# One group of attention value products is placed later in its cycle of steps

## The chip, the cores and the metric

The program runs on one core of one Trainium2 chip. The metric is the device time of one execution in microseconds (us), as the median of several runs. Lower is better.

## The reference, cut to what matters

Four blocks follow each other, each on a layer-normed input and with a residual: causal attention with ALiBi, a mixture-of-experts feed-forward on part of the rows, causal attention with rotary embedding, and the feed-forward again. Both attentions have 4 batches of 2048 rows of 256 features, 16 heads of 16. All is f32.

```
q, k, v = (x @ W.T + b), split into 16 heads of 16
scores  = q @ k.T * scale (+ alibi), masked to be causal
out     = softmax(scores) @ v           # the value products
x       = x + out @ Wo.T
```

Only the order in which one piece of `softmax(scores) @ v` is issued changes here. What is computed stays the same.

## The kernel before, in words

Each attention layer and batch (8 in all, "beta") has 16 heads, worked on as 8 pairs. So there are 64 head pairs, g = 0 to 63. One head pair is one pass over 36 steps, n = 0 to 35, in nine cycles of four steps. A pass takes about 54 us.

In one step and for one pair g, the following happens.

- **unit(g + 1, n)** on TensorE (PE, lines 1226, 1232 and 1239) multiplies queries by keys for the *next* head pair, both heads at once in the two halves of the array's rows. VectorE (DVE, line 1594) takes the row maxima out of PSUM. The products go to two pairs of banks in turn, so unit n waits (semaphore `p1_used`) until DVE has reduced unit n - 2. After unit 35 DVE also makes the negated maxima (lines 1601 to 1613).
- **score(g, n, u)** for u = 0 and 1 (lines 1196, 1200 and 1205) multiplies keys by queries for this head pair, with the maxima folded in. Each uses one bank of a ring of three, so it waits (`ring_used`) until the result three places before it has been taken out. ScalarE (ACT, line 1081) writes the exponential of it to `probs`.
- **times_v(g, group)** (line 1263), the value products, multiplies `probs` by the values of the steps of a group and adds them up in one PSUM bank, `ps_acc`. It waits for the last exponential of its group.
- After the last group of a block of 512 queries (qt) ACT copies `ps_acc` to `acc_sb` (line 1092, `acc_evac`), and SyncE's queue (SP) stores that copy with four DMAs (line 826, `store_o`). The first group of the next block waits for the copy (`acc_out`).

Steps run from qt = 3 down to qt = 0. The value groups are pairs of steps, and triples at the end of a block: group 14 is steps 30, 31 and 32 and ends block qt = 1; group 15 is steps 33, 34 and 35 and is the whole of block qt = 0. `value_slots` gives each group one of two value places per cycle, numbered k: the first place of a cycle is even, the second odd. Group 14 has place 16 and place 17 is empty; group 15 has place 18, which is place 0 of the next head pair.

Cycles are written out by hand in two orders. Where the cycle has a job for the ring (a projection, a transpose, an output product), which is so for the last cycle in 57 of the 64 head pairs, the last cycle on PE is, with n = 32:

```
unit 32; score(32,0); job; unit 33, masks first; score(32,1); score(33,0)
unit 34; score(33,1); PLACE 16; unit 35, masks first
score(34,0); score(34,1); score(35,0); PLACE 17; score(35,1), masks first
```

Without a job (g = 0, 57 and 59 to 63) it is:

```
unit 32; score(32,0); score(32,1); score(33,0); unit 33; PLACE 16
score(33,1), masks first; score(34,0); unit 34; score(34,1); score(35,0)
unit 35; score(35,1); PLACE 17
```

"Masks first" means that the small bf16 matmuls with the causal mask stand ahead of the large ones of that item. ACT goes through its exponentials in the same order, with the copy (`value_evac`) at the matching place: place 16 lies after exp(33,1), place 17 between exp(35,0) and exp(35,1) with a job and after exp(35,1) without. All engines run their own instruction list in order and wait on semaphores. After head pairs 31 and 60 (`EX_AFTER`) the experts' feed-forward follows, with group 15 ahead of it; after 63 comes the tail of the kernel.

Of the kernel before, what the change touches and what calls it, by code (L numbers as in the profile page):

```python
# [134 lines left out]
def value_slots():  # L135

    ready = [CYCLE * c + half for c in range(CYCLES + 1) for half in range(2)]
    found, k = {}, 0
    for i, steps in enumerate(GROUP):
        while ready[k] < steps[-1]:  # L140
            k += 1
        found[k], k = i, k + 1
    return found


GROUP_AT = value_slots()
assert len(GROUP_AT) == GROUPS and GROUP_AT[2 * CYCLES] == GROUPS - 1 and 0 not in GROUP_AT
LAST_GROUP = {qt: max(i for i, steps in enumerate(GROUP) if STEP[steps[0]][0][0] == qt) for qt in range(NQ)}
# [6 lines left out]
EX_AFTER = (NG // 2 - 1, NG - 4)  # L155
# [191 lines left out]
def build(nc, x_in, w_a, wo_a, bqk_a, bv_a, bo_a, w_b, wo_b, tri_in, ramp_in, cos_t, sin_t, rows_in_t,  # L347
# [12 lines left out]
    with ExitStack() as ctx:  # L360
# [219 lines left out]
        def evac_index(g, qt):  # L580
            return NQ * g + NQ - 1 - qt
# [5 lines left out]
        def step_width(n):  # L587
            return sum(QW - q0 for _, _, q0, _ in STEP[n])
# [37 lines left out]
        def _(sp):  # L626
# [189 lines left out]
            def store_o(g, qt):  # L816
                e = evac_index(g, qt)
                beta, p = divmod(g, PAIRS)
                sp.wait_ge(acc_out, e + 1)
                for u in range(2):  # L820
                    row = o_d[beta % 2, 2 * p + u, :, qt * QW:(qt + 1) * QW].rearrange("r (c n) -> r c n", n=P)
                    for inner in range(2):
                        to = row[:, 1:3, :] if inner else row[:, 0::3, :]
                        tile = 32 * (2 * u + inner)
                        src = acc_sb[tile:tile + DH + 1, e % ACCS, :].rearrange("p (c n) -> p c n", n=P)
                        sp.dma_start(to, src).then_inc(o_st[e % ACCS], 16)
# [27 lines left out]
            def experts(ly):  # L854
                sp.wait_ge(pv_mm, GROUPS * (EX_AFTER[ly] + 1))
                load_w2(w2_sb[0], expert_at(0), ew2_in[0])
                sp.wait_ge(qk_split, 2 * (unit_index(EX_UNITS[ly], NQ - 1, CH - 1) + 1))
                e = expert_at(1)
                load_w1(w1_sb[1], e, ew1_in[1])
                load_w2(w2_sb[1], e, ew2_in[1])  # L860
                sp.wait_ge(h_mm, (ly * ETILES + 1) * NF)
                sp.dma_start(xb[:, :, :], x_raw.rearrange("(t p) d -> p t d", p=P)).then_inc(xb_in, 16)
                for i in range(2, ETILES):
                    sp.wait_ge(h_mm, (ly * ETILES + i - 1) * NF)
                    e = expert_at(i)
                    load_w1(w1_sb[i % 2], e, ew1_in[i % 2])
                    sp.dma_start(xs_sb[:, i % 2, 0:HALVES[i], :], slots(xs, i)).then_inc(xs_in[i % 2], 16)
                    sp.wait_ge(fy_mm, halves_to(ly, i - 1))
                    load_w2(w2_sb[i % 2], e, ew2_in[i % 2])
                    store_ys(ly, i - 2)  # L870
                store_ys(ly, ETILES - 2)
                store_ys(ly, ETILES - 1)
# [32 lines left out]
            for g in range(NG):  # L905
                if g % PAIRS == 0 and g // PAIRS == B - 1:
                    sp.wait_ge(job_mm, JOB_PLACE[("v", B - 1, NQ - 1, CH - 1)] + 1)
                    sp.wait_ge(next_stored, 32)
                    for i, w in enumerate((wqkv, wqkv_low)):
                        sp.dma_start(w[:, :, :].bitcast(F32), w_d[i].rearrange("p (k n) -> p k n", k=KD))\  # L910
                            .then_inc(weights_in, 16)
                if g % PAIRS == 0 and g // PAIRS == B + 1:
                    sp.wait_ge(job_mm, JOB_PLACE[("y", B - 1, NQ - 1, CH - 1)] + 1)
                    sp.dma_start(wo[:, :, :], wo_b.rearrange("(k p) n -> p k n", p=P)).then_inc(wo_in, 16)
                for n in range(STEPS):
                    for j in JOBS[g][n]:
                        job(*j)
                    if g < NG - 1 and n % 2 == 0 and n >= 2 and GROUP_AT.get(n // 2 - 1) in LAST_QT:
                        store_o(g, LAST_QT[GROUP_AT[n // 2 - 1]])
                    if n == 2 and g and g - 1 not in EX_AFTER:  # L920
                        store_o(g - 1, 0)
                if g in EX_AFTER:
                    store_o(g, 0)
                    experts(EX_AFTER.index(g))
            job("zo", LAST, 3, 0)
# [878 lines left out]
```

## Time and profile before

| | us |
|---|---|
| runs, median of 3 | 3925.78 (3919.76 to 3927.37) |
| the profiled execution, time | 3912.85 |
| its span, first to last instruction | 3911.0 |
| PE busy / weight loads (PEld) busy | 3804.0 / 2394.0 |
| DVE busy / ACT busy | 2954.7 / 2759.7 |
| mean granted TensorE clock | 0.995 |

Durations below come from the profiled execution. Busy times overlap between engines. A busy PE is not PE at its peak, since the ends of matmuls are modelled.

### The profile page before, as it was taken

Reading aid. Unit: us, or ns where it says so; the run is one execution under the profiler, and the core shown is the slowest. Engines: PE = TensorE matmul, PEld = TensorE weight load, DVE = VectorE, ACT = ScalarE, POOL = GpSimd, SP = SyncE. Lnnn points to the kernel's source line nnn. Section 1 sums busy time; section 2 is a strip of 40 time slices with the busy share of each in tenths; the row PEclk is TensorE's granted clock in tenths of the full one; section 3 lists DMA queues with packets and bytes.
Section 4 is the critical chain, followed back from the end, with each engine's and each line's share of the span. In section 5 each row is a group of like instructions: output and inputs, shape, how many; then the busy total and the mean of one; then the engine's idle time right before and its main releaser. Section 6 shows DMA issues by size and latency. Waiting matters only on the chain.

```text
span 3911.0 us, 109334 instructions
## 1 busy us (share of the span) xinstructions
PE 3804.0 (97%) x42693; PEld 2394.0 (61%) x42693; DVE 2954.7 (76%) x3839; ACT 2759.7 (71%) x5702; POOL 1062.0 (27%) x1794
## 2 busy tenths in 40 slices
PE   7999999999999999999999999999999999999998
PEld 5555555655665655556875565655656555557955
DVE  8888888888888888885048888888888888883075
ACT  2777777777777777776257777777777777774265
POOL 4121112222222234442024433333343332120021
PEclk9999999999999999999999999999999999999999
DMA  5333233224333343335644334344333333336622
GB/s 165 77 76 92 56 79 91 73 77 97 78 87 92 93 114 94 92 104 170 229 138 117 95 89 102 92 105 105 90 99 99 83 90 89 73 83 196 232 68 83
DMA packets 275748, 407.05 MB, mean 104 GB/s; under 512 B 65226, under 2 KB 190098, under 8 KB 262418
## 3 DMA queue, kind: packets, MB, share of 16 engines
q1 hardware_dynamic: 272158, 391.66, 37.7%
q0 software_dynamic: 3072, 8.39, 0.8%
q8 instruction: 337, 5.52, 0.6%
q14 instruction: 181, 1.48, 0.1%
HBM read 264.70 MB, written 122.13 MB: 99 GB/s over the span
## 4 chain that ended last, share of the span: by engine, by line
PE 50%; DVE 2%; ACT 2%; issue 1%; SPq 1%; DMA 1%; POOL 0%; ACTq 0%; DVEq 0%
PE ps_acc L1263 14%; PE ps_r L1200 10%; PE ps_p L1232 9%; PE ps_p L1388 4%; PE ps_r L1400 4%; ACT probs L1081 2%; PE ps_r L1324 2%; DVE part_max L1594 1%; PE ps_r L1205 1%; PE ps_r L1309 1%; PE ps_p L1226 1%; PE ps_r L1319 1%; PE ps_r L1310 1%; PE ps_r L1311 1%; PE ps_p L1239 1%
## 5 line engine op out<-in xcount | busy, mean ns | idle before, releaser
L1594 DVE TENSOR_REDUCE part_max<-ps_p 128x2 f32<-128x1024 f32 (+3 forms) x2560 | 2623.1, 1060 | 567.6 <-PE ps_p L1232 375.8
L1081 ACT ACTIVATE probs<-ps_r 128x512 f32<-128x512 f32 (+1 forms) x4608 | 2333.9, 575 | 684.9 <-PE ps_r L1200 430.5
L1200 PE MATMUL ps_r<-q_stack,k_stack 54*128 54x512 f32 (+3 forms) x5120 | 1378.4, 392 | 37.9 <-ACT probs L1081 29.1
L1232 PE MATMUL ps_p<-k_stack,q_stack 52*128 52x512 f32 (+3 forms) x5120 | 1246.7, 427 | 20.2 <-DVE part_max L1594 17.7
L1263 PE MATMUL ps_acc<-probs,v_head 128*17 128x256 f32 x19456 | 1145.1, 360 | 1.8 <-ACT probs L1081 1.6
L1200 PEld LDWEIGHTS ps_r<-q_stack,k_stack 54*128 54x128 f32 x5120 | 733.4, 187 | 268.1 <-ACT probs L1081 219.5
L1263 PEld LDWEIGHTS ps_acc<-probs,v_head 128*17 128x17 f32 x19456 | 488.8, 97 | 467.5 <-issue 219.3
L1232 PEld LDWEIGHTS ps_p<-k_stack,q_stack 52*128 52x128 f32 x5120 | 557.8, 186 | 288.2 <-DVE part_max L1594 143.9
L1205 PE MATMUL ps_r<-id,mk 64*128 64x64 bf16 x3598 | 284.3, 194 | 0.0
L1715 DVE COPY xf<-ps_r 128x256 f32<-128x256 f32 x46 | 19.5, 424 | 316.1 <-PE ps_r L1400 316.1
L1032 POOL TENSOR_TENSOR bk<-bk,y_sb 128x256 f32<-128x256 f32 x104 | 76.4, 735 | 647.8 <-ACT y_sb L1132 647.7
L986 POOL TENSOR_TENSOR swp<-swp,cs 128x256 f32<-128x256 f32 x128 | 91.2, 735 | 546.2 <-ACT probs L1081 330.2
L1145 ACT ACTIVATE hid_f<-ps_p 128x256 f32<-128x256 f32 (+1 forms) x240 | 80.3, 334 | 220.6 <-PE ps_p L1388 220.6
L1205 PEld LDWEIGHTS ps_r<-id,mk 64*128 64x128 bf16 x3598 | 158.9, 95 | 87.6 <-issue 46.9
L995 POOL CAST pa<-tmp 128x512 fp32r<-128x512 f32 x128 | 78.6, 614 | 483.8 <-ACT tmp L1123 451.3
L1003 POOL CAST x_high<-xT 128x512 fp32r<-128x512 f32 x56 | 34.3, 612 | 599.3 <-ACT xT L1111 599.3
L998 POOL TENSOR_TENSOR pb<-tmp,pa 128x256 fp32r<-128x256 f32 x256 | 182.4, 734 | 10.3
L1400 PE MATMUL ps_r<-probs,hid_f 128*128 128x256 f32 x736 | 164.0, 379 | 1.1 <-issue 1.1
L1239 PE MATMUL ps_p<-id,mk 64*128 64x64 bf16 x2196 | 164.6, 195 | 0.0
L1092 ACT ACTIVATE acc_sb<-ps_acc 128x256 f32<-128x256 f32 x256 | 99.5, 389 | 76.9 <-PE ps_acc L1263 69.4
L1309 PE MATMUL ps_r<-x_high,wqkv 128*128 128x256 f32 x448 | 149.5, 334 | 0.0
L1400 PEld LDWEIGHTS ps_r<-probs,hid_f 128*128 128x128 f32 x736 | 137.6, 190 | 19.1 <-issue 1.3
(199 smaller groups left out, 3157.2 us busy)
## 6 DMA issues: line engine op xcount, KB each, us to landing
q_stack<-parts SPq DMA_DIRECT2D x378, 128.0 KB
k_stack<-parts SPq DMA_DIRECT2D x378, 128.0 KB
parts<-pa SPq DMA_DIRECT2D x128, 256.0 KB, 2.8
parts<-pb SPq DMA_DIRECT2D x128, 256.0 KB, 3.5
probs<-w_dram SPq DMA_DIRECT2D x30, 1024.0 KB, 6.1
o_sums<-acc_sb SPq DMA_DIRECT2D x1008, 17.0 KB
swp<-tmp SPq DMA_DIRECT2D x128, 128.0 KB, 3.3
bk<-recips SPq DMA_DIRECT2D x58, 256.0 KB
```

Of the source, the lines that this page charges most:

```text
L998: pool.tensor_tensor(pb[:, at % 2, h], x[:, h], pa[:, at % 2, h].bitcast(F32), ALU.subtract)\
L1081: act.activation(probs[:, at % PBUF, u, 0:w], block_bank(g, n, u)[:, 0:w], ACT.Exp)\
L1092: act.activation(acc_sb[:, e % ACCS, :], ps_acc[:, 0:D], ACT.Copy).then_inc(acc_out, 1)
L1200: mm = pe.matmul(bank[:, col:col + QW - q0], ks[s][r, kb * P:(kb + 1) * P], qs[s][r, qt * QW + q0:(qt + 1) * QW], start=fresh, stop=True, ...
L1205: mm = pe.matmul(bank[:, lo:lo + HALF], mk[half, 2 + part % 2, :], id64[half, :], start=False, stop=True, skip_group_check=True)
L1232: mm[u] = pe.matmul(banks[:, u, col:col + w], qs[s][r, qb * P:(qb + 1) * P], ks[s][r, kc * QW:kc * QW + w], start=fresh, stop=True, skip_g ...
L1239: mm[u] = pe.matmul(banks[:, u, lo:lo + HALF], mk[r, part % 2, :], id64[r, :], start=False, stop=True, skip_group_check=True)
L1263: mm = pe.matmul(ps_acc[tile:tile + DH + 1, to[0] * P:(to[-1] + 1) * P], v_head[:, beta % 2, kb, 2 * p + u, :], src, start=kb == 0, stop=n ...
L1309: pe.matmul(to[:, 0:D], wqkv[:, k, w], x_high[:, j, k, :], start=(k == 0), stop=False)
L1388: mm = pe.matmul(ps_p[:, f % 4, 0:n], w[k][:, f * P:(f + 1) * P], xsT[:, i % 2, k, 0:n], start=(k == 0), stop=(k == KD - 1))
L1400: mm = pe.matmul(y_bank[c], hid[:, f, c * P:(c + 1) * P], w2_sb[i % 2][:, f, :], start=(f == 0), stop=(f == NF - 1))
L1594: mm = dve.tensor_reduce(part_max[:, :, qb, kc], ps_p[:, p1_banks(g, n), col:col + w], AX_X, ALU.max)
```

## The change

Group 14 (steps 30 to 32) goes from place 16 to place 17. In `value_slots` a group may take an even place only if its last step lies before the cycle's first step; group 14 is the only group that had its last step there. The store of block qt = 1 was issued by SP at step 34, which no longer comes after the copy, and is now issued at step 0 of the next head pair, or ahead of the experts.

```diff
@@ -137,7 +137,7 @@
     for i, steps in enumerate(GROUP):
-        while ready[k] < steps[-1]:
+        while ready[k] < steps[-1] + (k % 2 == 0):
             k += 1
         found[k], k = i, k + 1
@@ -917,9 +917,12 @@
                         store_o(g, LAST_QT[GROUP_AT[n // 2 - 1]])
+                    if n == 0 and g and g - 1 not in EX_AFTER:
+                        store_o(g - 1, 1)
                     if n == 2 and g and g - 1 not in EX_AFTER:
                         store_o(g - 1, 0)
                 if g in EX_AFTER:
+                    store_o(g, 1)
                     store_o(g, 0)
```

## Rows read from the trace of the kernel before

**Rows 1.** The page: busy time and share of the span by engine.
```profile
PE 3804.0 (97%) x42693; PEld 2394.0 (61%) x42693; DVE 2954.7 (76%) x3839; ACT 2759.7 (71%) x5702; POOL 1062.0 (27%) x1794
```

**Rows 2.** The waits, whole span: engine, line, releaser, total us, times, longest.
```profile
PEld ps_r L1196 <- ACT probs L1081: 70.6, 176, 0.6
PE ps_r L1196 <- ACT probs L1081: 13.2, 56, 0.5
```

**Rows 3.** Groups by line, PE: value products, last number the idle time before.
```profile
L1263 PE MATMUL ps_acc<-probs,v_head 128*17 128x256 f32 x19456 | 1145.1, 360 | 1.8 <-ACT probs L1081 1.6
```

**Rows 4.** Timeline of PE, g = 10, last cycle: start, length, engine, line, count.
```profile
687.29 0.23 PE L1205 MATMUL ps_r<-id,mk 64*128 64x64 bf16 x2
687.45 1.28 PE L1263 MATMUL ps_acc<-probs,v_head 128*17 128x256 f32 x28
688.66 0.23 PE L1226 MATMUL ps_p<-id,mk 64*128 64x64 bf16 x4
...
689.56 0.42 PE L1205 MATMUL ps_r<-id,mk 64*128 64x64 bf16 x5
690.21 0.23 PE L1196 MATMUL ps_r<-id,mk 64*128 64x64 bf16 x2 [0.23 <-ACT probs L1081]
690.28 0.36 PE L1200 MATMUL ps_r<-q_stack,k_stack 54*128 54x256 f32 x1
690.32 0.56 PE L1232 MATMUL ps_p<-k_stack,q_stack 52*128 52x512 f32 x2
690.79 0.46 PE L1200 MATMUL ps_r<-q_stack,k_stack 54*128 54x512 f32 x1
691.19 0.39 PE L1319 MATMUL ps_r<-wqkv,x_high 128*128 128x256 f32 x1
...
692.43 0.40 PE L1200 MATMUL ps_r<-q_stack,k_stack 54*128 54x512 f32 x2
```

**Rows 5.** Timeline of ACT, same stretch.
```profile
686.77 1.45 ACT L1081 ACTIVATE probs<-ps_r 128x256 f32<-128x256 f32 x3 [0.25 <-PE ps_r L1205]
688.80 0.38 ACT L1092 ACTIVATE acc_sb<-ps_acc 128x256 f32<-128x256 f32 x1 [0.58 <-PE ps_acc L1263]
689.56 1.64 ACT L1081 ACTIVATE probs<-ps_r 128x512 f32<-128x512 f32 x4 [0.38 <-PE ps_r L1205]
```

**Rows 6.** Timeline of ACT, 689.6 to 690.0: exp(34,0) alone.
```profile
689.56 0.60 ACT L1081 ACTIVATE probs<-ps_r 128x512 f32<-128x512 f32 x1 [0.38 <-PE ps_r L1205]
```

**Rows 7.** Timeline of DVE, 686.6 to 687.5: the reduction of unit 33 alone.
```profile
686.59 1.23 DVE L1594 TENSOR_REDUCE part_max<-ps_p 128x2 f32<-128x1024 f32 x1 [0.71 <-PE ps_p L1232]
```

**Rows 8.** Timelines of DVE and PE around 680: unit 28's reduction, then unit 30.
```profile
678.81 1.23 DVE L1594 TENSOR_REDUCE part_max<-ps_p 128x2 f32<-128x1024 f32 x1 [0.80 <-PE ps_p L1232]
...
680.11 0.48 PE L1232 MATMUL ps_p<-k_stack,q_stack 52*128 52x512 f32 x2
```

**Rows 9.** Timeline of PE, g = 59, last cycle, which has no job.
```profile
3504.29 1.28 PE L1263 MATMUL ps_acc<-probs,v_head 128*17 128x256 f32 x28
3505.50 0.20 PE L1196 MATMUL ps_r<-id,mk 64*128 64x64 bf16 x1
...
3506.80 0.38 PE L1232 MATMUL ps_p<-k_stack,q_stack 52*128 52x256 f32 x1
...
3507.28 0.38 PE L1200 MATMUL ps_r<-q_stack,k_stack 54*128 54x256 f32 x1
...
3507.50 0.23 PE L1205 MATMUL ps_r<-id,mk 64*128 64x64 bf16 x2
3508.11 0.50 PE L1232 MATMUL ps_p<-k_stack,q_stack 52*128 52x512 f32 x2 [0.38 <-DVE part_max L1594]
```

**Rows 10.** Timeline of DVE, g = 59, 3504.4 to 3505.5: unit 33's reduction.
```profile
3504.34 1.23 DVE L1594 TENSOR_REDUCE part_max<-ps_p 128x2 f32<-128x1024 f32 x1 [0.26 <-PE ps_p L1239]
```

**Rows 11.** SP: what it waited for, and one store's four issues.
```profile
SPq L826 <- ACT acc_sb L1092: 856.1, 210, 16.0
...
1004.11 1.42 SPq L826 DMA_DIRECT2D o_sums<-acc_sb  x4
```

## The prediction

> **What bounds the kernel.** I read the page's busy shares first. PE is shown busy for 97% of the span, with no other engine above 76% [rows 1]. So whatever moves the time must move PE: work added to it, or time in which it has nothing it may issue. The change adds and removes no instruction on any engine. Only order changes, so its price is a difference of waits on PE.
>
> The list of waits came next. The value products themselves hardly wait: 1.8 us of idle time before all 19456 of them [rows 3]. So the place that group 14 has now isn't costly by a wait of its own. One wait, though, sits in just the stretch that is rearranged: the masks that open score(35,1) (L1196) wait for an exponential 56 times, 13.2 us in all [rows 2]. 56 is almost the number of head pairs whose last cycle has a job (57). In the other job cycles the masks-first score at this place has no mask.
>
> Then I read one last cycle in order of time, that of g = 10, engine by engine [rows 4 to 7]; the others with a job repeat it. PE ends the masks of score(33,1) (starts 687.29 and 687.33), runs group 14 from 687.45, and goes on with unit 35 at 688.66: the group holds PE for 688.66 - 687.45 = 1.21 us. Meanwhile ACT runs dry. It has finished exp(33,1) at 686.77 + 1.45 = 688.22, makes the copy at 688.80, and gets exp(34,0) only at 689.56. PE then issues the scores (34,0), (34,1) and (35,0) faster than ACT takes them out. Its last mask starts at about 689.56 + 0.42 - 0.19 = 689.79 (a single such mask lasts 0.19 to 0.20), and score(35,1) must wait for exp(34,0), which ends at 689.56 + 0.60 = 690.16 [rows 6]. It starts at 690.21, 0.05 after. Back to back, masks start about 0.04 apart (687.29 and 687.33), so the old wait costs PE 690.21 - 689.79 - 0.05 = 0.37 us per head pair.
>
> **The change, head pairs with a job (57).** Take group 14 out of its place. The next item is unit 35, which may start only when DVE has reduced unit 33. That reduction ends at 686.59 + 1.23 = 687.82 [rows 7]. Before, the group covered this time. How soon a released unit starts is seen at 680: the reduction ends at 680.04 and unit 30 starts at 680.11 [rows 8], 0.07 later; behind ACT it was 0.05. With masks first I take 0.05, so unit 35 starts at 687.87. PE could have had it at 687.33 + 0.05 = 687.38. This is a new wait of about 0.49 us, on DVE.
>
> From there I keep the distances of rows 4. Unit 35 to the last mask of score(35,0) took 689.79 - 688.66 = 1.13, so that mask starts at 689.00. None of the three scores waits for ACT in this stretch: ACT has finished exp(33,1), the last that they need, at 688.22, and score(35,0), the one that needs it, comes after 688.5. Masks to value products took 687.45 - 687.33 = 0.12, so group 14 starts at 689.12 and gives PE back 1.21 later, at 690.33. Score(35,1) needs exp(34,0), which now ends near 688.77 + 0.60 = 689.37, so the old wait is gone. It starts at 690.33 instead of 690.21: **0.12 us later**. The same sum, new wait minus old wait, is 0.49 - 0.37. Over 57 head pairs, at 0.11 (the same replay elsewhere gives 0.10 or 0.11), it is 57 x 0.11 = 6.3 us.
>
> What follows score(35,1) is a close chain on PE (690.28, 690.32, 690.79, 691.19 in rows 4) that shows no wait, so I let it shift whole.
>
> **ACT.** The copy now stands between exp(35,0) and exp(35,1). It waits for the group's end: 689.12 + (688.80 - 687.45) = 690.47, and lasts 0.38, to 690.85. Score(35,1) is ready for its exponential at about that time too (690.33 + 0.07 + 0.36 + 0.09 = 690.85; the 0.09 is like the copy's delay behind the last value product). So exp(35,1) ends at 691.25, against 689.56 + 1.64 = 691.20 now. The first to need its bank is score(0,1) of the next head pair, near 692.43. Slack 1.2 us: cost nothing. Without that cover the copy would cost its 0.38.
>
> **SP and the store.** Four issues take 1.42 us [rows 11]. The block's store moves past the jobs of steps 34 and 35 and the ring job's followers at step 0; the queue then stands until the copy's end, 690.85, and is free near 692.3. Behind it stand at most a row load or a rotary swap of steps 1 and 2, and then the store of block 0, which waits for a later copy in any case. SP stood 210 times for such copies anyway [rows 11]. Each buffer of `acc_sb` is used again only three copies on. Cost nothing; bound 1.4 us on a swap whose reader is on POOL, 27% busy.
>
> **Head pairs without a job (7).** Here the group stands right behind exp(32,1), and in g = 59 unit 0 of the next pass then waits for DVE [rows 9]. After the change DVE's unit 33 ends at 3504.34 + 1.23 = 3505.57 [rows 10], so unit 35 may start at 3505.62 instead of 3506.80. Score(35,1) came 0.48 after it, 3506.10; its last mask some 0.25 later, near 3506.35; the group 0.12 behind and 1.21 long ends at 3507.68 (3505.50 - 3504.29 is 1.21 here too). Unit 0 starts there instead of at 3508.11, 0.43 earlier. For g = 57, 59 and 61 that is -1.3 us, for 0 and 62 some -0.8 together, and for 60 and 63, where group 15 or the tail waits for the copy instead, -0.4: together -2.5 us.
>
> **Sum.** +6.3 - 2.5 = +3.8 us on a profiled 3912.85 us. That execution lies 12.9 us under the median of 3925.78, and I carry the difference over unchanged: 3925.8 + 3.8 = 3929.6. What a measurement of this kernel can tell from no change is about 0.2%, or 7.9 us, so this is no change that can be told.
>
> **How large the old wait is: a page weighed against rows.** The trace prints 0.23 us of idle PE before L1196 in rows 4, measured from the previous matmul's end, and 13.2 us in all. Start to start I found 0.37, and I use starts for both waits, so that the two are measured alike. By the printed 0.23 against 0.49 the sum would be 57 x 0.26 = +14.8, less 2.5, or +12.3. The Trainium skill (Perfetto Trace Analysis, section Tensor Engine Instruction) says that the end of a matmul in the profile is estimated from its size and not observed, which speaks for starts too.
>
> **Rivals.**
> - *The new wait is no wait* (faster). If unit 35 could start at 687.38, or its wait were covered, only the old wait's removal would be left: 57 x -0.37 - 2.5 = -23.6, 3902. For it: 70.6 us of idle weight loads before L1196 [rows 2] are given back. Against it: 680.11 in rows 8, a unit held until its reduction ends. It decides if the unit starts more than 0.2 us before the reduction's end plus 0.05.
> - *The copy holds ACT* (slower). By the code's order exp(35,1) stands behind the waiting copy. If the copy's 0.38 came onto PE's path it would cost 57 x 0.38 - 2.5 = +19.2, 3945. Against it stands the slack of 1.2 us; it decides only when exp(35,1) ends later than score(0,1) asks, at 692.5. The Trainium skill (TensorE: Matmul & The Clock Gate, section Architectural detail) has ScalarE as a strict first-in first-out queue; rows 5 agree, with a copy that waits 0.58 us and nothing passing it.
> - *The place itself costs more* (slower). The group now stands between scores of different row halves, and the next unit 0 has no mask to go first. If each head pair lost 0.1 more, the sum is 57 x 0.21 - 2.5 = +9.5, 3935. It decides beyond 0.18 per head pair.
> - *The 0.11 is absorbed* (no change). DVE itself stood idle for PE by 0.71 and 0.80 us [rows 7, 8], so it can catch up, and some later unit may be bound by an event that didn't shift. Then only -2.5 is left, 3923.
>
> **How the numbers follow.** Forecast, new wait a little longer than the old: 0.49, 3929.6, its own range 3924 to 3934. Absorbed: 0.23. Place costs more: 0.15. Copy holds ACT: 0.06. No wait: 0.07. Same takes the first two less 0.03 for the lower tail: 0.69. Faster is 0.07 + 0.03 = 0.10, slower 0.15 + 0.06 = 0.21. The range of 8 in 10 reaches to the absorbed and the costlier case with 4 to 5 us for the medians: 3919 to 3940.
>
> **What the changed profile would show.** At each last cycle with a job: unit 35's masks (L1226) start 0.05 after DVE's reduction of unit 33, with a wait of PE on DVE; the waits of L1196 on ACT fall from 13.2 us to nearly nothing; the 28 value products stand directly ahead of L1196; exp(34,0) comes 0.8 us earlier against unit 33; and L1196 starts 3.74 us after unit 33's reduction began (690.33 - 686.59), where it was 3.62. The prediction is wrong if L1196 starts before 3.5 or after 3.9, or if score(0,1) waits for exp(35,1).

## The result, and the profile after

The kernel takes 3906.92 us after the change (median of 13 runs, 3901.55 to 3914.81). The kernel before took 3915.23 us beside it on the same chip (median of 13, 3912.37 to 3927.37). The ratio is 0.9969, with a 95% interval of 0.9960 to 0.9979. So the change makes the kernel faster by 0.31%, or 12 us (8 to 16; the two medians differ by 8.3). I had forecast 3.8 us slower. The profiled execution took 3905.41 us, with a span of 3903.6 us against 3911.0, at nearly the same granted clock (0.996 against 0.995).

Three lines are new ahead of everything below, so each line number of PE, ACT and DVE is 3 higher: L1196 is L1199, L1200 is L1203, L1226 is L1229, L1263 is L1266.

The page after the change, the first part, as in [rows 1]:

```profile
PE 3789.0 (97%) x42693; PEld 2380.3 (61%) x42693; DVE 2949.6 (76%) x3839; ACT 2762.4 (71%) x5702; POOL 1061.8 (27%) x1794
```

The groups by line of PE with their forms apart, after (the numbers behind the bar are busy us, mean ns of one, and the idle time before with its releaser):

```profile
L1229 PE MATMUL ps_p<-id,mk 64*128 64x64 bf16 x1900 | 90.0, 194 | 19.4 <-DVE part_max L1597 19.4
L1199 PE MATMUL ps_r<-id,mk 64*128 64x64 bf16 x498 | 46.4, 194 | 0.1
```

Both waits moved as forecast. The masks of score(35,1) no longer wait for ACT: 0.1 us is left, where 13.2 us stood in [rows 2]. The masks of the units (L1229) now wait for DVE by 19.4 us. The list of waits counts them (total us, times, longest):

```profile
PE ps_p L1229 <- DVE part_max L1597: 19.4, 57, 0.3
```

That is once per head pair with a job. By these two rows alone PE lost 6 us. Yet it won. So the gain must lie behind L1199, and I read the same last cycle, g = 10, again.

The timeline of PE after:

```profile
687.16 0.23 PE L1229 MATMUL ps_p<-id,mk 64*128 64x64 bf16 x4 [0.35 <-DVE part_max L1597]
...
688.05 0.42 PE L1208 MATMUL ps_r<-id,mk 64*128 64x64 bf16 x5
688.41 1.28 PE L1266 MATMUL ps_acc<-probs,v_head 128*17 128x256 f32 x28
689.62 0.20 PE L1199 MATMUL ps_r<-id,mk 64*128 64x64 bf16 x1
689.63 0.49 PE L1235 MATMUL ps_p<-k_stack,q_stack 52*128 52x512 f32 x1
689.66 0.19 PE L1199 MATMUL ps_r<-id,mk 64*128 64x64 bf16 x1
689.68 0.36 PE L1203 MATMUL ps_r<-q_stack,k_stack 54*128 54x256 f32 x1
689.89 0.39 PE L1235 MATMUL ps_p<-k_stack,q_stack 52*128 52x512 f32 x1
689.96 0.39 PE L1203 MATMUL ps_r<-q_stack,k_stack 54*128 54x512 f32 x1
690.28 0.39 PE L1322 MATMUL ps_r<-wqkv,x_high 128*128 128x256 f32 x1
```

The timeline of DVE after, the reduction of unit 33 alone:

```profile
685.87 1.23 DVE L1597 TENSOR_REDUCE part_max<-ps_p 128x2 f32<-128x1024 f32 x1 [0.71 <-PE ps_p L1235]
```

The reduction ends at 687.10 and unit 35 starts at 687.16. The value products stand directly ahead of L1199, which starts at 689.62, 3.75 us after the reduction began. I had forecast 3.74, against 3.62 before. Up to here the forecast holds to 0.01 us.

What comes behind L1199 is score(35,1), then unit 0 and score(0,0) of the next head pair, then its first job. Measured from the start of the masks of score(35,1), by [rows 4] and the rows above:

| | before | after |
|---|---|---|
| score(0,0) | 690.79 - 690.21 = 0.58 | 689.96 - 689.62 = 0.34 |
| the job | 691.19 - 690.21 = 0.98 | 690.28 - 689.62 = 0.66 |

The stretch is 0.32 us shorter. Less the 0.12 that L1199 comes later, the head pair ends 0.20 earlier. Score(0,0) had a wait of its own before, and it shows in the weight loads.

The timeline of PE's weight loads before, from score(35,1) to the job:

```profile
690.25 0.19 PEld L1200 LDWEIGHTS ps_r<-q_stack,k_stack 54*128 54x128 f32 x1
690.32 0.23 PEld L1232 LDWEIGHTS ps_p<-k_stack,q_stack 52*128 52x128 f32 x2
690.76 0.18 PEld L1200 LDWEIGHTS ps_r<-q_stack,k_stack 54*128 54x128 f32 x1 [0.21 <-issue]
```

The same after, cut to 689.85 to 689.95:

```profile
689.73 0.19 PEld L1203 LDWEIGHTS ps_r<-q_stack,k_stack 54*128 54x128 f32 x1
```

Before, the weights of score(0,0) start to load at 690.76, 0.03 before its matmul, with 0.21 us of idle time ahead of them. After, they load at 689.73, 0.23 before it. The timeline of ACT before, cut to 690.3 to 690.5, has the exponential that lies between, exp(34,1):

```profile
690.06 0.59 ACT L1081 ACTIVATE probs<-ps_r 128x512 f32<-128x512 f32 x1
```

Exp(34,1) ends at 690.65, and score(0,0) stands three places behind score(34,1) in the ring, so it uses the same bank. The trace also holds the instruction that waits for `ring_used` (line 1190) ahead of score(0,0). Line 1190 before, from 690.2 to 691:

```profile
L1190 PEldq EVENT_SEMAPHORE  x1: 51/51/51, 690.7 to 690.7; - x1
```

The same line after, from 687 to 690.2:

```profile
L1193 PEldq EVENT_SEMAPHORE  x1: 51/51/51, 689.2 to 689.2; - x1
```

Before, the wait is passed right after exp(34,1)'s end (690.65) and 0.06 us ahead of the weight load. After, exp(34,1) ends at 689.14, the wait is passed at 689.2, and the weights load only 0.5 us later, at their turn. So before the change PE waited twice for ACT in nearly all of these head pairs, once for exp(34,0) and once for exp(34,1): score(0,0) starts 0.14 us after the end of exp(34,1) in 52 of the 57. The profile put the second wait down to "issue", and the list of waits names no releaser for it:

```profile
PEld ps_r L1200 <- issue: 15.4, 67, 0.8
```

After the change this row is down to 4.0 us and 16 times. The timeline of ACT after has exp(34,0), exp(34,1) and exp(35,0) in one row:

```profile
688.06 1.36 ACT L1084 ACTIVATE probs<-ps_r 128x512 f32<-128x512 f32 x3 [0.55 <-PE ps_r L1208]
```

All three end by 689.42, 0.54 us before score(0,0) starts, so neither wait is left.

Over the whole trace (the starts of the exponentials of score(32,0) and score(0,0) compared between the two traces), 47 of the 57 head pairs with a job are 0.18 to 0.20 us shorter in their last cycle. Of the other ten, g = 24, 27, 28 and 40 are 0.22, 0.12, 0.26 and 0.46 shorter, and nearly the same in the kernel with the job pairs alone (below). G = 12, 20, 36, 44 and 52, which differ by +0.16 to +1.03, differ by up to 0.5 to 1.1 in kernels that don't touch this place, and g = 31 (-0.26) stands ahead of the experts.

### The profile page after: what moved, and what is told of

Same layout as the page of the kernel before. It is cut to its first block, busy times and chain, and to the rows that moved or that the text cites. A ratio compares the mean times of both kernels' runs of the same rounds, so it can differ in the third digit from the quotient of the medians.

```text
span 3903.6 us, 109334 instructions
## 1 busy us (share of the span) xinstructions
PE 3789.0 (97%) x42693; PEld 2380.3 (61%) x42693; DVE 2949.6 (76%) x3839; ACT 2762.4 (71%) x5702; POOL 1061.8 (27%) x1794
## 4 chain that ended last, share of the span: by engine, by line
PE 49%; DVE 3%; ACT 2%; issue 1%; SPq 1%; DMA 1%; POOL 0%; ACTq 0%; DVEq 0%
PE ps_acc L1266 14%; PE ps_r L1203 10%; PE ps_p L1235 9%; PE ps_p L1391 4%; PE ps_r L1403 4%; DVE part_max L1597 2%; PE ps_r L1327 2%; ACT probs L1084 1%; PE ps_r L1208 1%; PE ps_r L1312 1%; PE ps_p L1229 1%; PE ps_r L1322 1%; PE ps_r L1313 1%; PE ps_r L1314 1%; SPq L826 1%
## 5 line engine op out<-in xcount | busy, mean ns | idle before, releaser
L1203 PE MATMUL ps_r<-q_stack,k_stack 54*128 54x512 f32 (+3 forms) x5120 | 1369.2, 391 | 40.1 <-ACT probs L1084 27.9
L1235 PE MATMUL ps_p<-k_stack,q_stack 52*128 52x512 f32 (+3 forms) x5120 | 1251.1, 428 | 20.8 <-DVE part_max L1597 17.7
L1266 PE MATMUL ps_acc<-probs,v_head 128*17 128x256 f32 x19456 | 1144.2, 360 | 1.1 <-ACT acc_sb L1095 0.6
L1203 PEld LDWEIGHTS ps_r<-q_stack,k_stack 54*128 54x128 f32 x5120 | 728.2, 187 | 258.4 <-ACT probs L1084 220.1
L1266 PEld LDWEIGHTS ps_acc<-probs,v_head 128*17 128x17 f32 x19456 | 489.0, 97 | 466.4 <-issue 216.8
L1235 PEld LDWEIGHTS ps_p<-k_stack,q_stack 52*128 52x128 f32 x5120 | 561.9, 185 | 296.6 <-DVE part_max L1597 153.3
L1403 PEld LDWEIGHTS ps_r<-probs,hid_f 128*128 128x128 f32 x736 | 137.6, 190 | 19.4 <-issue 1.1
```

Of the source, the lines that this page charges most:

```text
L1203: mm = pe.matmul(bank[:, col:col + QW - q0], ks[s][r, kb * P:(kb + 1) * P], qs[s][r, qt * QW + q0:(qt + 1) * QW], start=fresh, stop=True, ...
L1235: mm[u] = pe.matmul(banks[:, u, col:col + w], qs[s][r, qb * P:(qb + 1) * P], ks[s][r, kc * QW:kc * QW + w], start=fresh, stop=True, skip_g ...
L1266: mm = pe.matmul(ps_acc[tile:tile + DH + 1, to[0] * P:(to[-1] + 1) * P], v_head[:, beta % 2, kb, 2 * p + u, :], src, start=kb == 0, stop=n ...
L1403: mm = pe.matmul(y_bank[c], hid[:, f, c * P:(c + 1) * P], w2_sb[i % 2][:, f, :], start=(f == 0), stop=(f == NF - 1))
```

## The experiments

In the table each kernel is compared with the kernel before on the same chip. "Last cycle" is what the last cycle of a head pair with a job lost or gained against it (median).

| kernel | us | ratio (95%) | last cycle, us |
|---|---|---|---|
| job pairs alone | 3904.35 | 0.9972 (0.9961 to 0.9983) | -0.19 |
| pairs without a job alone | 3915.78 | 0.9995 (0.9985 to 1.0005) | 0.00 |
| store alone | 3917.53 | 0.9994 (0.9985 to 1.0004) | 0.00 |
| after, one score ahead of unit 35 | 3893.26 | 0.9941 (0.9928 to 0.9953) | -0.53 |
| before, exp(34,0) longer | 3965.64 | 1.0029 (1.0017 to 1.0040) | +0.17 |
| after, exp(34,0) longer | 3945.75 | 0.9978 (0.9966 to 0.9989) | -0.19 |
| before, reduction of unit 33 longer | 3953.15 | 1.0000 (0.9989 to 1.0011) | 0.00 |
| after, reduction of unit 33 longer | 3958.40 | 1.0012 (1.0000 to 1.0024) | +0.14 |
| before, exp(34,1) longer | 3929.91 | 1.0028 (1.0017 to 1.0040) | +0.18 |
| before, one score ahead of unit 35 | 3911.91 | 0.9992 (0.9980 to 1.0005) | -0.13 |
| after, one score ahead in every job cycle | 3894.52 | 0.9943 (0.9930 to 0.9957) | -0.54 |
| after, not ahead of a transpose | 3904.14 | 0.9968 (0.9955 to 0.9981) | -0.19 |

The kernel before was 3916.22 us beside the first four, 3952.13 beside the next four, which ran on a slower chip, and 3918.07 beside the last four.

### Which part carries the gain

The first two kernels make the change in only some head pairs. `value_slots` is computed for both placements, and each head pair picks one:

```diff
+def late(g):
+    return has_job(g, 32)          # the other kernel: not has_job(g, 32)
+
+def group_at(g):
+    return LATE_AT if late(g) else EARLY_AT
```

> Group 14 goes to the later place only in the 57 head pairs whose last cycle has a job; in the 7 others it stays at the first place. Theory A (two waits of TensorE for ScalarE, before score(35,1) and before score(0,0), are exchanged for one shorter wait for VectorE before unit 35): 0.20 us less in 44 pairs and about 0.09 us more in the 13 that go on to a transpose job, so -7.5 us, ratio 0.998; the trace has the masks of score(35,1) 0.1 us later and score(0,0) 0.12 us earlier against exp(32,0) than before. Rival B (the gain is in the cycles without a job, and the others pay the 0.11 us of the prediction): +6 us, ratio 1.0015. Rival C (the gain comes from the store's later place in SyncE's queue): as the changed kernel, 0.997.

> The complement: the later place only in the 7 head pairs whose last cycle has no job. Theory A: -0.5 to -0.6 us each in five of them and less at the experts and the tail, -2.9 us in all, ratio 0.9993. Rival B: -12 us or more, ratio 0.997. Rival C: next to nothing, as only 7 stores move.

The job pairs alone give 0.9972, nearly all of the 0.9969, and a gain of 11 us where my prediction had a loss of 6.3. The pairs without a job give 0.9995, whose interval holds both nothing and the 2.5 us of the prediction. The trace sees more. In the pairs without a job the last cycles of g = 0, 57, 59 and 61 are 0.50, 0.55, 0.61 and 0.62 us shorter, that of g = 62 is 0.09 shorter.

The third kernel leaves group 14 where it was and makes only SP's store of block qt = 1 late, at step 0 of the next head pair:

```diff
+                    if n == 0 and g and g - 1 not in EX_AFTER:
+                        store_o(g - 1, 1)
+                    if g < NG - 1 and n % 2 == 0 and 2 <= n < 34 and GROUP_AT.get(n // 2 - 1) in LAST_QT:
```

> Group 14 and its copy stay at the first place; only the store of block 1 is issued where the changed kernel issues it, at step 0 of the next head pair. Theory A: nothing, ratio 1.000 within 0.001, and the last cycle on TensorE as before. Rival C (SyncE's queue): ratio 0.997.

It does nothing that can be measured, and the old wait is all there, as the group of the masks of score(35,1) shows:

```profile
L1199 PE MATMUL ps_r<-id,mk 64*128 64x64 bf16 x498 | 46.5, 194 | 13.4 <-ACT probs L1084 13.1 <-DVE part_max L1597 0.2
```

So the gain is in PE's order, in the head pairs with a job.

### Which event each stretch waits for

Five kernels make one supposed releaser later. An extra exponential of 128 columns, or an extra maximum over 2 x 128 columns, stands ahead of the real one, in head pairs with a job, and writes a tile that nobody reads:

```diff
+                if n == 34 and u == 0 and has_job(g, 32):    # u == 1 for exp(34,1)
+                    act.activation(zeros[:, :], block_bank(g, n, u)[:, 0:P], ACT.Exp)
...
+                    if n == 33 and g and has_job(g - 1, 32):
+                        dve.tensor_reduce(spare_max[:, :], ps_p[:, p1_banks(g, n), col:col + P], AX_X, ALU.max)
```

> The kernel before, with one more exponential of 128 columns of the same bank (into a tile that nobody reads) ahead of exp(34,0), in the 57 pairs with a job. Theory A: exp(34,0) and exp(34,1) are what TensorE waits for before score(35,1) and score(0,0), so what the extra one takes (0.16 to 0.27 us by the spacing of exponentials) is added in full: the masks of score(35,1) start that much later, +9 to +15 us, ratio 1.003. Rival D (ScalarE isn't on the path here): ratio 1.000.

> The same extra exponential in the changed kernel. Theory A: both waits for ScalarE are gone, with some 0.9 us of slack before score(35,1) and 0.6 us before score(0,0), so it costs nothing: the ratio stays that of the changed kernel, 0.997. Rival E (ScalarE is still what the path waits for, by the copy of the accumulator behind group 14): it adds 9 to 15 us, ratio 1.000.

> The kernel before, with one more reduction of 128 columns of both heads (into a tile that nobody reads, about 0.4 us) ahead of the reduction of unit 33, in the 57 pairs with a job. Theory A: group 14 covers it, since unit 35 starts 0.85 us after the reduction of unit 33 ends; at most little is lost further on: ratio 1.000 to 1.001.

> The same extra reduction in the changed kernel. Theory A: unit 35 waits for this reduction with nothing in between, so unit 35, group 14 and the masks of score(35,1) come 0.4 us later in each of 57 pairs: +23 us, ratio to the kernel before 1.003. Rival D (the new wait is covered or is not on the path): ratio 0.997 to 0.998.

These four bear out the exchange of waits. With a longer exp(34,0), the kernel before loses 0.29%, and the kernel after nothing that can be told (0.9978, where it was 0.9969 without it, with intervals that overlap; in the trace its last cycle is still 0.19 shorter). With a longer reduction it is the other way round: before 1.0000, after 1.0012 and a last cycle longer by 0.14 + 0.19 = 0.33 us, which is what the reduction ends later. I had expected 0.4 us and a ratio of 1.003. The groups by line of that last kernel:

```profile
L1230 PE MATMUL ps_p<-id,mk 64*128 64x64 bf16 x1900 | 90.0, 194 | 38.4 <-DVE part_max L1600 38.4
```

The new wait is twice the 19.4 us of the kernel after, longer by 19.0 / 57 = 0.33 us each time. So DVE's reduction sets the last cycle after the change, and exp(34,0) did before.

They say nothing yet of score(0,0), whose wait I had by then only read off a gap. The fifth kernel touches exp(34,1) alone, which score(35,1) doesn't need:

> The kernel before, with the extra exponential of 128 columns ahead of exp(34,1) instead of exp(34,0), in the 57 pairs with a job. It can't touch the wait of score(35,1), which is for exp(34,0). Theory A (score(0,0) of the next pair has a wait of its own, for exp(34,1)): the masks of score(35,1) and unit 0 stay where they are against exp(32,0), and score(0,0) comes 0.18 us later; +8 to +10 us, ratio 1.0025. Rival F (score(0,0) follows unit 0 by TensorE's own work and waits for nothing, as the prediction had it): nothing moves, ratio 1.000.

The timeline of ACT, exp(34,0), the extra one, and exp(34,1) and the next two:

```profile
693.18 0.60 ACT L1083 ACTIVATE probs<-ps_r 128x512 f32<-128x512 f32 x1 [0.38 <-PE ps_r L1207]
693.67 0.27 ACT L1082 ACTIVATE zeros<-ps_r 128x128 bf16<-128x128 f32 x1
693.83 1.16 ACT L1083 ACTIVATE probs<-ps_r 128x512 f32<-128x512 f32 x3
```

The timeline of PE in the same kernel:

```profile
693.83 0.23 PE L1198 MATMUL ps_r<-id,mk 64*128 64x64 bf16 x2 [0.23 <-ACT probs L1083]
693.90 0.36 PE L1202 MATMUL ps_r<-q_stack,k_stack 54*128 54x256 f32 x1
693.94 0.56 PE L1234 MATMUL ps_p<-k_stack,q_stack 52*128 52x512 f32 x2
694.58 0.47 PE L1202 MATMUL ps_r<-q_stack,k_stack 54*128 54x512 f32 x1
```

The masks stand where they stood, 693.83 - 693.18 = 0.65 us after exp(34,0) starts (690.21 - 689.56 = 0.65 in [rows 4, 6]). Score(0,0) comes 694.58 - 693.83 = 0.75 us after them, where it was 0.58. The kernel is slower by 0.28%, or 11 us; 57 x 0.18 is 10 us. The wait of score(0,0) for `ring_used` is now passed at 694.5, again right after exp(34,1), which ends at 693.83 + 0.61 = 694.44. This shows the second wait: what exp(34,1) ends later, the head pair ends later.

### What the new wait costs, and its cover

If DVE's reduction is what unit 35 waits for, PE should do something else first. Score(34,0) needs nothing that DVE makes:

```diff
                         value_slot(g, n // 2)
+                        if n == 32:
+                            score(g, n + 2, 0)
                         unit(g + 1, n + 3, masks_first=True)
-                        score(g, n + 2, 0)
+                        if n < 32:
+                            score(g, n + 2, 0)
                         score(g, n + 2, 1)
```

> The changed kernel, with score(34,0) put ahead of unit 35 in the last cycle of head pairs with a job. Theory A says that after the change unit 35 waits 0.45 us for VectorE's reduction of unit 33 and that score(34,0) is free to go at that time: the wait is filled, 0.3 to 0.35 us less per pair in 57 pairs, some -18 us against the changed kernel, ratio to the kernel before 0.992. Rival D (that wait isn't on the path, since ScalarE's exponentials set the pace from exp(34,0) on): nothing against the changed kernel, ratio 0.997.

This is the fastest kernel of the study: 0.9941, and its interval doesn't touch that of the change. The timeline of PE in its cycle of g = 10:

```profile
687.92 0.23 PE L1229 MATMUL ps_p<-id,mk 64*128 64x64 bf16 x4
...
688.83 1.28 PE L1266 MATMUL ps_acc<-probs,v_head 128*17 128x256 f32 x28
690.04 0.20 PE L1199 MATMUL ps_r<-id,mk 64*128 64x64 bf16 x1
```

The timeline of DVE in the same kernel, the reduction of unit 33 alone:

```profile
686.64 1.23 DVE L1600 TENSOR_REDUCE part_max<-ps_p 128x2 f32<-128x1024 f32 x1 [0.71 <-PE ps_p L1235]
```

Unit 35 shows no idle time before it any more, but it isn't free of DVE: it still starts 0.05 us after the reduction's end, 686.64 + 1.23 = 687.87. What is new is that a score runs in the time of the wait and no longer stands behind it. From unit 35 to L1199 it is 690.04 - 687.92 = 2.12 us, against 689.62 - 687.16 = 2.46 in the kernel after. That is 0.34 less, and the last cycle is 0.53 - 0.19 = 0.34 shorter. Over 57 head pairs that is 19 us, which is what I expected (ratio 0.992). The two ratios lie only 0.28% apart, or 11 us, give or take 6, so part of the 19 isn't seen in the time, and no run shows where it goes.

Is it the swap alone that gains? The same edit on the kernel before, and the swap in every job cycle on the kernel after:

> The kernel before (group 14 at the first place), with score(34,0) put ahead of unit 35. Theory A: exp(34,0) comes 0.25 us earlier, so the old wait before score(35,1) shrinks from 0.37 to 0.1 us; exp(34,1) follows, so the wait before score(0,0) shrinks too: 0.2 to 0.3 us less per pair, -15 us, ratio 0.996. If it reaches the 0.994 of the kernel with both edits, the group's move is worth nothing once the order is so.

> The changed kernel, with score(n+2,0) ahead of unit n+3 in every cycle with a job and not only in the last. In the other cycles a group stands at the first place and covers VectorE's reduction, so there is no wait to fill before unit n+3, but exponentials start earlier. Theory A: at least as fast as with the last cycle alone, ratio 0.990 to 0.994. Rival: the mask-free unit then pays its weight load and the cycles get longer, ratio 0.996 or more.

Without the move the swap gives 0.9992, no difference that can be told, and my expectation was wrong. It makes the masks of score(35,1) 0.17 us earlier, but score(0,0) then still waits for exp(34,1), so the last cycle gives only 0.13, and part of that is lost again in the next cycle (below). In the last cycle swap and move together give more than the sum of both (0.53 against 0.13 + 0.19), since the move takes the two waits for ACT away and the swap covers the wait for DVE that the move brings. In the other job cycles it gives nothing: 0.9943 against 0.9941, with one of those cycles 0.16 us shorter and another 0.11 longer.

### What is given back

After 13 of the head pairs with a job the next one begins with a transpose job, and in 12 of them its cycle 0 is 0.28 us longer after the change (behind the thirteenth, g = 31, stand the experts, and nothing changes). I took g = 9. The timeline of PE before, from its score(35,1) into the next head pair:

```profile
636.67 0.23 PE L1196 MATMUL ps_r<-id,mk 64*128 64x64 bf16 x2 [0.23 <-ACT probs L1081]
...
638.23 0.50 PE L1232 MATMUL ps_p<-k_stack,q_stack 52*128 52x512 f32 x2
...
638.80 0.42 PE L1232 MATMUL ps_p<-k_stack,q_stack 52*128 52x512 f32 x2
...
639.42 0.84 PE L1263 MATMUL ps_acc<-probs,v_head 128*17 128x256 f32 x14
```

The same after:

```profile
637.24 0.50 PE L1235 MATMUL ps_p<-k_stack,q_stack 52*128 52x512 f32 x2
...
638.03 0.50 PE L1235 MATMUL ps_p<-k_stack,q_stack 52*128 52x512 f32 x2
...
638.70 1.06 PE L1266 MATMUL ps_acc<-probs,v_head 128*17 128x256 f32 x20
```

And the timeline of DVE after, the reduction of unit 0:

```profile
636.75 1.23 DVE L1597 TENSOR_REDUCE part_max<-ps_p 128x2 f32<-128x1024 f32 x1 [0.58 <-PE ps_p L1235]
```

From unit 1 to unit 2 it is now 638.03 - 637.24 = 0.79 us, where it was 638.80 - 638.23 = 0.57. Unit 2 starts 0.05 us after 636.75 + 1.23 = 637.98, the end of unit 0's reduction: PE gained on DVE, and has to wait for it at the next place. The kernel that leaves the late place out in the head pairs ahead of a transpose job tests this:

```diff
+def late(g):
+    return not (g + 1 < NG and any(j[0] == "xt" for j in JOBS[g + 1][0]))
```

> The changed kernel, but with group 14 left at the first place in the 14 head pairs whose successor begins with a transpose job. Theory A: those pairs lose 0.09 us each by the change, since unit 2 of the next pass waits for VectorE's reduction of unit 0, which starts 0.11 us later; leaving them out saves 1.2 us against the changed kernel, too little for the times: ratio 0.9967. The trace has cycle 0 after them unchanged against before. If the change helped them too, the ratio goes towards 0.998.

In its trace the last cycle of those head pairs and the cycle 0 after them are as before (0.00 and 0.00, but for g = 31, whose last cycle, ahead of the experts, differs from run to run). It leaves out 13 head pairs, not the 14 that I had counted. The sum was to be no more than 12 x (0.28 - 0.19) = 1.1 us, and the ratio, 0.9968, can't tell it from the change. So the give-back is shown in the trace, and its worth in time isn't.

This kernel doesn't touch seven more head pairs that give back as well. Behind g = 2, 3, 4, 26, 55, 56 and 58 the next cycle 0 is 0.19 to 0.31 us longer, 1.6 us in all, in this kernel as in the kernel after. Behind g = 2, 4 and 26 it is the same wait: unit 2 starts 0.05 to 0.06 us after the end of unit 0's reduction. Behind the other four the next cycle has no job, and no run shows the cause.

## Why the prediction was wrong, point by point

- **The new wait.** Unit 35 starts 0.06 us after the end of DVE's reduction (0.05 forecast), and waits 57 times. Right, in mechanism and size.
- **The old wait.** 13.2 us of L1196 behind ACT fall to nothing. Right. L1199 comes 3.75 us after the reduction's start (3.74). The sum of new less old, 0.11 to 0.12 us per head pair, is what the traces show.
- **The step that failed** is the one behind it, the overlap of PE and ACT behind score(35,1), put at nothing: "What follows score(35,1) is a close chain on PE (690.28, 690.32, 690.79, 691.19 in rows 4) that shows no wait, so I let it shift whole." It doesn't shift whole. It held a second wait for ACT, 0.24 us (0.58 - 0.34) before score(0,0), and 0.08 more before the job (0.98 - 0.58 = 0.40, now 0.66 - 0.34 = 0.32). Both go when ACT does its exponentials of step 34 earlier, which I had forecast myself. So each last cycle gives 0.12 - 0.32 = -0.20 us and doesn't cost 0.11. The wait for exp(34,1) is shown by the kernel that makes exp(34,1) longer. The 0.08 in front of the job was not tested by itself. The profile names ACT ahead of the job's weights before the change (0.24 us of idle time, ended at 691.18), but exp(35,0), whose bank the job takes, had ended at 690.92, 0.26 earlier, where the weights of score(0,0) come 0.11 after their releaser. The job keeps 0.39 to 0.40 in the kernels in which score(0,0) waits and 0.32 in those in which it doesn't, so the 0.08 goes with that wait; why is open.
- **Could it be read?** Yes. In [rows 4] score(0,0) starts 0.47 us after unit 0's first matmul, and after the change 0.33 (689.96 - 689.63). By [rows 5, 6] exp(34,1) ends between exp(34,0)'s end at 690.16 and 691.20. The wait on line 1190, passed at 690.7, could be read too. I had asked of the ring only who waits for exp(34,0), and not who waits for the next one. Both scores wait three places back, and ACT was late for both. The Trainium skill (TensorE: Matmul & The Clock Gate, section Architectural detail: the array is 16x 32x32, not 1x 128x128) says that PE's queue can pull weight loads ahead of running matmuls. The two timelines of weight loads agree: 0.23 us ahead without a wait, 0.03 us with one. That was a hint and no proof: the job's weights after the change start with their matmul too (690.28), with 0.32 us of "issue" before them, and their bank had been free since 689.42.
- **Head pairs without a job.** Forecast -0.43 for g = 57, 59 and 61; measured -0.55, -0.62 and -0.62. Right in sign, a little small. For g = 0 and 62 together -0.61 against -0.8, and 0.24 more in the cycle behind g = 62. G = 60 differs by -0.5 to +0.4 in kernels that leave it alone, so that one can't be read.
- **ACT and SP at nothing.** Right: the copy and exp(35,1) hold nobody, and the store alone gives 0.9994 (0.9985 to 1.0004).
- **The base.** The forecast of 3929.6 adds 3.8 us to 3925.78, a median of 3 runs. Beside the changed kernel the kernel before took 3915.23 (13 runs). So of the 22.7 us between 3929.6 and 3906.92, 10.6 lie in the base and say nothing of the change, and 12.1 (3.8 forecast, -8.3 measured) belong to the failed step.
- **A premise that cost nothing.** "In the other job cycles the masks-first score at this place has no mask" isn't so: score(23,1) has two masks. In g = 10 they start at 671.51, with no idle time before them.
- **The rivals.** "The 0.11 is absorbed" went the right way for the wrong reason: nothing absorbs it, another wait is taken away. "The new wait is no wait" doesn't hold, although its time, 3902, is nearest to the 3906.92 measured. That nearness is luck, from the base: as a difference it had -23.6 us, where 8 to 16 were gained. Of the 70.6 us of idle weight loads that it counted on, 62.7 are still there. "The copy holds ACT" and "the place itself costs more" don't hold.

The sum with the step put right: 57 x -0.195 = -11.1, then +3.4 given back behind 12 of these (0.28 each) and +1.6 behind seven more, and -2.6 for the five pairs without a job that can be read. That is -8.7 us, or -0.22%. It lies within the measured -0.31% (-0.40 to -0.21), near its edge; the two medians differ by 8.3 us and the profiled spans by 7.4. For the job pairs alone the same sum is -6.1 us, where the ratio says -11 (-7 to -15). So the like cycles show the sign and most of the size, and a few us that the ratios add aren't located.

## What to carry to other kernels

When a buffer ring is the limit, a late releaser holds more than one waiter: having found the first, put every later user of the ring against the event that frees its own place, before letting a stretch "shift whole". Idle time put down to "issue" ahead of a weight load is worth the same question as a named wait, and the time at which the wait on the semaphore was passed answers it. And a move that exchanges one wait for another is half a change: the work that now stands behind the new wait may go in front of it, which here was worth about as much again as the move.

## What the runs showed of the hardware

- A waiting score starts later after its release than waiting masks do. The masks start 0.05 us after the exponential's end (690.16 to 690.21); score(0,0), which has no mask, begins to load its f32 weights 0.11 after it (690.65 to 690.76) and starts 0.14 after (690.65 to 690.79, and 693.83 + 0.61 = 694.44 to 694.58 in the kernel with the longer exp(34,1), whose real exponential starts at 693.83 and lasts 0.61).
- A short operation costs less than its record. The extra exponential is 0.27 us long in the trace, and what follows comes 0.18 us later; the extra maximum lasts 0.42, and the reduction ends 0.33 later.
- Matmuls of the two row halves need not start in the listed order. In the timeline after, one of unit 0's two matmuls (L1235) starts at 689.63, before the second mask (689.66) and the score (689.68), which are listed ahead of it. The Trainium skill (TensorE: Matmul & The Clock Gate, section The mechanism) says that matmuls start and end strictly in program order. The starts here don't; the ends in the profile are modelled and can't tell.
